# Far probability tiles turned by VectorE blocks and on-chip transfers instead of by TensorE

## The reference, cut to what matters

```python
q = q * cos + _rotate_half(q) * sin
k = k * cos + _rotate_half(k) * sin
scores = jnp.einsum('bhqd,bhkd->bhqk', q, k) / math.sqrt(HD)
scores = jnp.where(causal[None, None], scores, jnp.finfo(jnp.float32).min)
probs = jax.nn.softmax(scores.astype(jnp.float32), axis=-1).astype(q.dtype)
out = jnp.einsum('bhqk,bhkd->bhqd', probs, v)
out = out.transpose(0, 2, 1, 3).reshape(b, s, H * HD)
return out @ wo + bo
```

## Time and profile before

| what | value |
|---|---|
| median of three runs | 1116.94 us |
| span of the profiled execution, first to last instruction | 1115.4 us |
| its own time on the device | not listed beside it; the three runs lie 1.3 to 2.9 us above the span |
| TensorE busy, weight loads | 1105.2 us, 1006.7 us |
| VectorE, ScalarE, GpSimd busy | 834.9, 748.3, 638.1 us |
| share of the closing chain on TensorE | 95% |
| transfers inside the chip, `work` to `work` | 256 of 128 KB |

### The profile page before, as it was taken

The page is one execution under the profiler, slowest core; times in us unless marked ns, Lnnn a source line. Parts: engine busy times, 40 slices in busy tenths (PEclk is TensorE's granted clock), DMA queues, the critical chain, the costliest instruction groups (busy, mean ns, idle before and its releaser), DMA issues.

```text
span 1115.4 us, 20396 instructions
## 1 busy us (share of the span) xinstructions
PE 1105.2 (99%) x7100; PEld 1006.7 (90%) x7100; DVE 834.9 (75%) x1978; ACT 748.3 (67%) x1584; POOL 638.1 (57%) x516
## 2 busy tenths in 40 slices
PE   9999999999999999999999999999999999999997
PEld 8999899999999999999999999999999999988897
DVE  7776777777777777777777777777777777977776
ACT  5666867666666666666666666666666666688765
POOL 2217666555555555555555555555555556777676
PEclk9999999999999999999999999999999999999999
DMA  5002412121212121212121212121211212230102
GB/s 176 1 1 62 129 39 53 39 62 39 52 39 62 39 53 39 60 39 50 37 60 39 52 39 62 39 48 44 62 38 37 50 40 57 48 110 14 39 1 76
DMA packets 33285, 56.54 MB, mean 51 GB/s; under 512 B 5792, under 2 KB 10016, under 8 KB 33184
## 3 DMA queue, kind: packets, MB, share of 16 engines
q1 hardware_dynamic: 33040, 55.21, 19.9%
q10 hardware_dynamic: 144, 0.03, 0.0%
HBM read 17.47 MB, written 4.19 MB: 19 GB/s over the span
## 4 chain that ended last, share of the span: by engine, by line
PE 95%; POOL 2%; issue 1%; ACT 1%; DMA 1%; DVE 1%; SPq 0%; POOLq 0%; ACTq 0%; DVEq 0%
PE ps_m L458 58%; PE ps_s L458 23%; PE ps_t L608 12%; PE ps_m L505 1%; DMA work<-in_attn_w 0%; POOL acc L2341 0%; POOL qk_lo L2346 0%; PE ps_m L479 0%; POOL wqk_lo L2346 0%; PE ps_t L458 0%; POOL pT_lo L2354 0%; DMA work<-work 0%; POOL acc L2330 0%; PE ps_m L666 0%; PE ps_m L667 0%
## 5 line engine op out<-in xcount | busy, mean ns | idle before, releaser
L2296 POOL TENSOR_TENSOR work<-work,rope 128x512 f32<-128x512 f32 x128 | 165.5, 1293 | 222.8 <-DMA work<-work 222.7
L1784 DVE TENSOR_TENSOR pT_lo<-ps_t,pT_hi 128x512 fp32r<-128x512 f32 (+3 forms) x408 | 210.8, 551 | 32.7 <-ACT pT_hi L1201 30.2
L1201 ACT ACTIVATE pT_hi<-ps_t 128x512 fp32r<-128x512 f32 (+3 forms) x408 | 182.8, 489 | 65.3 <-PE ps_t L608 65.1
L1777 DVE CUSTOM_DVE_ANT_0 ps_s<-ps_s,causal 128x128 f32<-128x128 f32 (+7 forms) x272 | 203.5, 767 | 6.7 <-PE ps_s L458 4.1
L2300 POOL TENSOR_TENSOR work<-work 128x512 f32<-128x512 f32 x128 | 167.6, 1310 | 10.0
L2307 POOL TENSOR_TENSOR qk_lo<-work,qk_hi 128x512 fp32r<-128x512 f32 x128 | 163.0, 1293 | 17.8 <-ACT qk_hi L1158 17.8
L1152 ACT ACTIVATE work<-ps_m,bqk 128x512 f32<-128x512 f32 x128 | 88.8, 694 | 116.5 <-PE ps_m L458 116.4
L1817 DVE SCALAR_TENSOR_TENSOR acc<-ps_m,rinv,acc 128x256 f32<-128x256 f32 x272 | 118.6, 478 | 63.0 <-PE ps_m L458 61.7
L1194 ACT ACTIVATE prob_b<-ps_s,nmax 128x640 f32<-128x640 f32 (+3 forms) x136 | 130.3, 958 | 17.9 <-DVE nmax L1777 14.6
L458 PE MATMUL ps_s<-qk_hi 128*128 128x384 f32 (+5 forms) x384 | 140.6, 366 | 0.0
L1738 DVE SCALAR_TENSOR_TENSOR work<-ps_m,bqk,rope 128x512 f32<-128x512 f32 x128 | 95.5, 746 | 54.3 <-ACT work L1152 54.0
(11 more groups left out here) (235 smaller groups left out, 2822.7 us busy)
## 6 DMA issues: line engine op xcount, KB each, us to landing
work<-work SPq DMA_DIRECT2D x256, 128.0 KB, 2.3
wst<-in_head_qk SPq DMA_DIRECT2D x16, 256.0 KB, 2.9
acc<-in_x_tiles SPq DMA_DIRECT2D x8, 256.0 KB, 6.8
wo_st<-in_L_ffn_wo SPq DMA_DIRECT2D x16, 128.0 KB, 2.4
wst<-in_pair_v SPq DMA_DIRECT2D x8, 256.0 KB, 3.0
x_rows<-acc SPq DMA_DIRECT2D x4, 512.0 KB, 3.6
wst<-in_expert SPq DMA_DIRECT2D x8, 256.0 KB, 3.0
rope<-x_rows SPq DMA_DIRECT2D x4, 512.0 KB, 4.1
```

Source lines behind the costliest of these rows:

```text
L1201: act.activation(pT_hi[:, slots, cols], t_bank(u, i, j)[:, 0:size * P].rearrange("p (j q) -> p j q", q=P), ACT.Copy).then_inc(t_hi.sem, t_ ...
L1777: dve.tensor_tensor_reduce(s, s, causal[:, T - (i + 1) * P:T], -1.0, ABOVE_ALL, ALU.add, ALU.min, accum_out=nmax[:, u % 2, i:i + 1]).then_ ...
L1784: dve.tensor_tensor(pT_lo[:, slots, cols], t_bank(u, i, j)[:, 0:size * P].rearrange("p (j q) -> p j q", q=P), pT_hi[:, slots, cols].bitcas ...
L2296: pool.tensor_tensor(qs[:, x % 2, :], qs[:, x % 2, :], sin_t[:, c * CH:(c + 1) * CH], ALU.mult).then_inc(sin_done.sem, sin_done.up(u, x))
```

## The change: what it does

It concerns units 3 to 30 (28 units, `FAR_UNITS`) and in them the 16 far tiles.

- TensorE turns only the near tiles (`groups_of`): 20 in place of 36 in a unit.
- `turn_far(u, i)`, i = 4 to 7, is a new VectorE instruction: it reads the far part of `prob_b` (128x512) with a step of four words and writes it, turned in blocks of 32x32, to `turned`. That is a 128x2048 buffer which shares its memory with the layer norm's `rows` and `hf`. `exponent` of the tile two further on, which writes over the same row of `prob_b`, now waits for it as well.
- `exchange(u)` is new on SP: when all four are turned and `outputs(u, 0)` is done, four transfers of 256 KB inside the chip. Each reads 32 partitions and writes one quarter of `pT_lo`, 128 partitions, in rows of 2 KB. It stands behind `swap(u + 1, 2)` and in front of `swap(u + 1, 3)`.
- `high_far` (ACT) and `low_far` (DVE), two each in a unit, split what arrived, 128x1024 at a time. `low_far` reads `pT_lo` and `pT_hi` and writes `pT_lo` in place. Both are in ordinary on-chip memory, not in a bank of TensorE's.
- `outputs(u, 1)` becomes `near_outputs(u)` (key tiles 4 to 7) and two `far_outputs(u, k)`, each of which waits for its `low_far`. Products and their sizes are the same 24; the columns lie in another order (by quarter, tile, query), which `high_p`, `low_p`, `high_o` and `low_o` follow with their access patterns.
- The order of `head(u)` is new on TensorE, ScalarE, VectorE and SP. On GpSimd nothing moves.

```diff
 def transposes(u, i):
     pe.wait_ge(exp_done.sem, exp_done.at(u, i))
-    for j, size in enumerate(TG[i]):
+    for j, size in groups_of(u, i):
...
+def near_outputs(u):
+    out = take_bank("pv", u, 1).rearrange("p (g q) -> p g q", g=4)
+    pe.wait_ge(v_lo_done.sem, v_lo_done.at(values_of(u), 3))
+    pe.wait_ge(t_lo.sem, t_lo.at(u, 7, 1))
...
+def far_outputs(u, k):
+    out = m_bank("pv", u, 1)
+    pe.wait_ge(far_lo.sem, far_lo.at(u, k))
+    for j in (2 * k, 2 * k + 1):
+        high, low = (x[:, 0:4, j * P:(j + 1) * P] for x in (pT_hi, pT_lo))
+        last = product(out, ..., (high, low), False, j == TC - 1)
...
 def exponent(u, i):
...
+    if before in turn_done.place:
+        act.wait_ge(turn_done.sem, turn_done.at(*before))
...
+def high_far(u, k):
+    act.wait_ge(exchanged.sem, exchanged.at(u))
+    act.activation(far_part(pT_hi, k), far_part(pT_lo, k).bitcast(F32), ACT.Copy)
...
+def turn_far(u, i):
+    dve.wait_ge(exp_done.sem, exp_done.at(u, i))
+    dve.transpose(out=turned[:, :, :, i - 4, :].rearrange("p g m q -> p m g q"),
+                  in_=prob_b[:, i % 2, 0:CH].rearrange("p (m k g) -> p m g k", g=4, k=Q4))
...
+def low_far(u, k):
+    dve.wait_ge(far_hi.sem, far_hi.at(u, k))
+    dve.tensor_tensor(far_part(pT_lo, k), far_part(pT_lo, k).bitcast(F32), far_part(pT_hi, k).bitcast(F32), ALU.subtract)
...
+def exchange(u):
+    sp.wait_ge(turn_done.sem, turn_done.at(u, NT - 1))
+    sp.wait_ge(pv_mm.sem, pv_mm.at(u, 0))
+    for g in range(4):
+        sp.dma_start(pT_lo[:, g, :].bitcast(F32), turned_by_keys[g * Q4:(g + 1) * Q4, :, :])
...
 def head(u):                        # SP
     swap(n, 2)
+    exchange(u)
+    swap(n, 3)
...
-    swap(n, 3)
```

More of the change, by code:

```diff
@@ L66, with is_far, groups_of @@
 VALUES = values_of(LAST) + 1
+FAR_UNITS = range(3, LAST - 2)
+FAR = 4 * CH
+Q4 = 32
 QK_JC = ((0, 0), (1, 0), (0, 1), (1, 1))
 TG = [[i + 1] if i < 4 else [4, i - 3] for i in range(NT)]
+def is_far(u):
+    return u in FAR_UNITS
+def groups_of(u, i):
+    return [(1, i - 3)] if is_far(u) and i >= 4 else list(enumerate(TG[i]))
 LN_VECTORS = (0, 0, 1, 1, 2, 2)
@@ L413, in m_bank, with o_bank, o_cols @@
             return ps_m[:, shared[use] % 2, :]
+        def o_bank(u, c):
+            out = m_bank("pv", u, c)
+            return out.rearrange("p (g i q) -> p i g q", g=4, i=4) if c and is_far(u) else out
+        def o_cols(x, u, c):
+            return x[:, :].rearrange("p (i g q) -> p i g q", g=4, i=4) if c and is_far(u) else x[:, :]
         def swap_of(u, x):
@@ L629, in outputs @@
                 tiles = TC * (c + 1)
+                early = 4 if c == 0 and not is_far(u) else 0
                 for j in range(tiles):
@@ L857, in head @@
                 out_project(u - 1, 1, 1)
-                project_q(n, 1)
+                transposes(u, 4)
+                scores(u, 7)
                 outputs(u, 0)
-                transposes(u, 4)
+                transposes(u, 5)
                 project_q(n, 2)
[L862 to L865, removed]
+                transposes(u, 6)
                 project_q(n, 3)
-                project_v(v_next, 2 * half_of(u))
                 scores(n, 0)
-                transposes(u, 6)
                 scores(n, 1)
                 scores(n, 2)
+                out_project(u, 0, 0)
+                transposes(u, 7)
+                out_project(u, 0, 1)
+                project_v(v_next, 2 * half_of(u))
                 scores(n, 3)
-                transposes(u, 7)
                 project_v(v_next, 2 * half_of(u) + 1)
-                outputs(u, 1)
+                near_outputs(u)
+                far_outputs(u, 0)
+                far_outputs(u, 1)
             def ends():
@@ L1402, in head @@
                     high_o_weights(p + 1, 0)
-                exponent(n, 0)
-                high_qk(n, 2)
-                high_qk(n, 3)
-                exponent(n, 1)
-                exponent(n, 2)
+                high_p(n, 0)
+                high_o(u, 1)
                 exponent(n, 3)
-                high_values(v_next, 2 * half_of(u) + 1)
-                high_o(u, 1)
-                high_p(n, 0)
                 high_p(n, 1)
```

154 lines of the change are left out of this document (102 added, 52 removed).

## The result

The changed kernel is 14% slower: 1275.56 us (median of 4 runs, 1274.27 to 1280.12) against 1117.63, ratio 1.1422, 95% interval 1.1400 to 1.1443. Its profiled execution took 1275.78 us, with a span of 1273.9. Forecast were 1138 us and at most 1152: the sign was right, the size was not, by 138 us.

The account below looks back on a forecast made before the run. The prediction took TensorE, busy 99% of the span, as the bound: 1116.9 us less 48.8 saved gives 1068.1, plus 28 new waits of 2.5 us gives 1138 us; range 1079 to 1152, the forecast's own 1122 to 1152.

Parts of the forecast that it names:

- TensorE's saving: On TensorE, 16 transposes go in each of 28 units: 1.74 us a unit, 48.8 us in all.
- 28 x 2.5: TensorE's new wait of 2.5 us, returning in each of 28 units, added to 1068.1 us to give 1138 us.
- The end of the path: From the exchange's landing to `transposes(n, 1)`: splits, GpSimd's work and an exponent make TensorE wait 2.5 us a unit.
- the start: `high_o(u, 0)` runs from 11.9 us after the unit's start; the exchange starts at 15.4 us, behind `swap(n, 2)`.
- the rate: The exchange's bytes move at 210 GB/s, 4 x 262 KB in 5.0 us, landed at 22.0 us in the unit.
- the fast rival: Exchange at 399 GB/s, landed at 19.4 us; `low_far` ends 0.4 us late, 1079 us; chance 0.22.
- the lock: VectorE and GpSimd exclude each other on instructions with two on-chip inputs: the later waits for the whole of the other.
- my third rival: Longer path: GpSimd's sine gets in 0.1 us before `low_far(u, 0)`, 3.0 us late, 1152 us; chance 0.12.
- The floor of 1068: The time with TensorE's saving and no new wait: 1116.9 - 48.8 = 1068.1 us.
- The turn: `turn_far` on VectorE taken at 0.69 us, with bounds of 0.5 and 1.29 us.
- its sign: What would show the forecast in the profile, for VectorE's turn: `turn_far` should be under 1 us.
- is not the bound by its load: VectorE's load rises from 20.9 to 23.4 us a unit, or 25.8 at the upper price, under 26.5.

## Why the prediction was wrong

- **TensorE's saving** was right: 49.1 us measured, 48.8 forecast.
- **The step that failed is the wait: "28 x 2.5"** in "The end of the path", and with it the range. A unit without waits was to take 28.20 - 1.74 = 26.46 us; it takes 33.9 on the mean, 7.4 more, not 2.5. Of the 7.4, 134.0 / 28 = 4.8 us are waits (3.1 for `low_far`, 1.0 for `low_o`, 0.5 for an exponent) and 73.6 / 28 = 2.6 are the same work taking longer, for which the sum had no term. Its mechanism, the exchange followed by `low_far` and GpSimd, was there, and so the sign was not luck; four terms of it were short or missing.
- First, **the start**. I had `high_o(u, 0)` run at 11.9 us and the exchange start at 15.4. In the units without weights that nearly came true (12.0 to 12.7 and 15.7 to 16.4 us, between 480 and 890 us of the run). In the others the exchange starts after 19.4 to 21.6 us: I looked only at what came after `high_o` in ScalarE's list, not at the `high_qk(n, 1)` ahead of it and of `exponent(u, 7)`, which waits for GpSimd. TensorE waits in these units for the PSUM bank as well, 2.4 and 1.7 us in turn. That wait by itself is 30 us (with no transfers, 1160.92 to 1131.08); under the exchange it is hidden. No run moves the start of an undivided exchange by itself.
- Second, **the rate**. "I take 210 GB/s": the stretch has 211, but the exchange ends 8.1 us after its first issue rather than 6.6. I had the bytes of `swap(n, 3)` run behind the exchange's. From 600.6 to 607.4 us the transfers moved 194 GB/s, 1.32 MB, and the exchange is only 1.05 MB of that (an estimate from the stretch and the sizes), so `swap`s ran beside it. The four issues alone take 4.18 us, and 2.49 when 128 partitions are read, so it seems that slow transfers hold up the queue. Reading from 32 partitions cost 88 us in all, by the test with a wide source. The rule on ports and the row agreed; I gave the fast rival 0.22. Its own sum was short too: with the wide source the time is 1187.56 us, not 1079.
- Third, **the lock** was priced for one meeting. The `swap` behind the exchange came at the same moment, so `low_far` met the sine, the add and a `low_qk`: 4.25 us for two, where my layout had 3.7 with the sine between them. In both units shown the first `low_far` already met the sine, which is the case of my third rival (chance 0.12). Under the exchange its share was not measured by itself (with the `swap` first, `low_far` took 1.22 us and the time did not fall); without transfers the lock is worth 24 us (1160.92 to 1137.19).
- Fourth, **the clock** was not in the sum at all. The earlier trace rows show a clock of 9 in all slices because TensorE never waited there; that it would stay so is what I had assumed without saying. With it TensorE's busy time is 73.6 us above what was due; with the clock held it is 37 less, of which 15 show in the time.
- **The waits at the weights** (13.6 us for the exponent that stands behind their splits, and 8.2 for `low_qk_weights` where there were no transfers) were in no part of the prediction: I laid out a unit without weights to split, and half of the units have them.
- **The floor of 1068** was reached by none: 1110.67 is the best. TensorE is busy 1079.3 us there, 23 more than 1056.1 though the clock is full, and idle 28.5.
- **The turn** was 1.10 us, inside its bounds, but above the value taken and above the 1 us that its sign asked for; it does not matter (1278.77 without the step).
- **VectorE "is not the bound by its load"** held: it is busy 77% of the span, and there is no wait at `near_outputs`.

What stays open: why 20 us more of TensorE's busy time than due are left at full clock (1076.4 with no transfers and the earlier `high_o`). In the groups by shape 7.1 of them lie on the high x high products of the projections (256 of 512 columns: 103.6 us before, 110.7 there), the rest is spread. Open is also what the low clock costs by itself, since it was not measured apart from the waits that bring it.

## What to carry to other kernels

A transfer on the path that is needed late in a stage can be cut by what is ready early: with half of it sent once its sources were done, and the splits moved along with it, 110 of 158 us went, while each cure of a single step (a faster turn, an earlier `swap`, a held clock, an earlier split) gave 0 to 15. The partitions that it reads matter as much, where the layout leaves a choice: 128 in place of 32 were worth 88 us, though with other bytes than this kernel needs. An edit that takes work from the bound engine leaves the lists of the others written for the old pace: look in each list at what stands ahead of the instruction that the bound engine waits for, in the stages with extra work too. And the bound engine's full clock in the profile was there while it never waited: where a change brings new waits of 2 to 3 us, price the products behind them at half speed too (so it was behind 24 of 28 waits for `low_far`, and behind two to five of seven waits of 2.4 us). Of that price only a part, here 15 of 37 us, may show in the time.

## What the runs showed of the hardware

- Behind most waits of 2.4 to 3.1 us TensorE's granted clock fell to half, the 1.2 GHz level, and came back only after 2.6 to over 5 us of products at 0.43 us for 512 columns. Behind waits of 3 us and more for `low_far` it fell in 14 of 16 cases; behind those of 2.4 us for `low_o` in two of seven in the changed kernel and in five of seven without transfers. With waits of at most 1.6 us (no transfers and the earlier `high_o`) it stayed full. Sixteen transposes of 0.109 us inside the wait kept it at 2.4 GHz behind 27 of 28 waits for `low_far`.
- On-chip to on-chip in rows of 2 KB: 32 partitions read by each transfer 211 GB/s, 128 read 337 GB/s. Four issues on SP's queue took 4.1 to 4.3 us in the first case and mostly 2.5 in the second.
- A VectorE turn of 128x512 in 32x32 blocks takes 0.69 us read densely and 1.09 with a step of 4 words.
- A VectorE subtraction of 128x1024 takes 1.22 us, and 2.26 to 2.29 at the median where GpSimd works beside it and both inputs are on chip; with one in PSUM it stays at 1.22.
